# Picking embedding rows by one-hot products: tables in teams of two, with shared compares and two banks

## The reference

```python
e = jnp.stack([tbl_0[ids[:, 0]], ..., tbl_31[ids[:, 31]]], axis=1)   # 512 x 32 x 128
dot = jnp.einsum('bnd,bmd->bnm', e, e)
z = dot[:, iu, ju]                                                   # pairs above the diagonal
h = jnp.concatenate([z, dense_ctx], axis=1)                          # 512 x 512
h = jnp.maximum(h @ W_top1 + b_top1, 0.0)
h = jnp.maximum(h @ W_top2 + b_top2, 0.0)
y = h @ W_top3
```

## Time and profile before

| what | value |
|---|---|
| runs shown | 124.79, 125.47, 125.48 us, median 125.47 |
| span of the profiled execution | 148.7 us |
| own time of the profiled execution | not listed; the runs shown are other executions |
| TensorE (matmul) busy | 121.4 us, 82% of the span, 1028 instructions |
| ScalarE busy | 78.8 us, 53%, 79 instructions |
| VectorE busy | 75.2 us, 51%, 196 instructions |
| GpSimd busy | 71.3 us, 48%, 76 instructions |
| mean granted TensorE clock | 0.919 |

### The profile page before, as it was taken

How to read it: one execution, slowest core, us unless ns; L and a number is a source line. 1 busy time by engine, 2 the same in 40 slices (tenths; PEclk the granted TensorE clock), 3 DMA queues, 4 the chain that set the end, 5 groups by cost and what they waited for, 6 DMA issues and landing times.

```text
span 148.7 us, 2677 instructions
## 1 busy us (share of the span) xinstructions
PE 121.4 (82%) x1028; PEld 99.5 (67%) x1028; DVE 75.2 (51%) x196; ACT 78.8 (53%) x79; POOL 71.3 (48%) x76
## 2 busy tenths in 40 slices
PE   5889979989999689499995464321999899999993
PEld 3457758868788468378884452111999798999971
DVE  2999999989897399496800000000333033223301
ACT  3588899999997897799950510000143302210022
POOL 3877749787787477378775577772000000000000
PEclk9999999999999999959999776555599999999999
DMA  5998736666667356793221011211056441024000
GB/s 144 275 338 267 234 100 204 204 216 225 217 219 235 110 178 195 232 324 113 55 53 52 23 53 53 53 53 35 4 146 202 136 126 35 4 78 127 10 0 1
DMA packets 11150, 19.81 MB, mean 133 GB/s; under 512 B 2353, under 2 KB 7473, under 8 KB 11138
## 3 DMA queue, kind: packets, MB, share of 16 engines
q1 hardware_dynamic: 7522, 13.74, 29.8%
q0 software_dynamic: 2176, 4.46, 10.3%
q10 hardware_dynamic: 1440, 1.44, 3.0%
HBM read 17.54 MB, written 2.13 MB: 132 GB/s over the span
## 4 chain that ended last, share of the span: by engine, by line
PE 64%; ACT 15%; issue 11%; another core or an unknown queue 5%; DVE 2%; DMA 2%; ACTq 0%
PE two_ps L564 15%; PE two_ps L566 14%; PE two_ps L606 8%; PE two_ps L625 8%; ACT onehot L442 8%; PE free_ps L606 7%; ACT emb L421 5%; PE free_ps L636 3%; PE turn_ps L574 3%; PE two_ps L636 2%; ACT high L421 2%; DMA id_sb<-row_ids 2%; PE two_ps L641 1%; PE turn_ps L625 1%
## 5 line engine op out<-in xcount | busy, mean ns | idle before, releaser
L307 POOL DMA_INDIRECT rows<-tables,row_no x64 | 66.6, 1040 | 26.5 <-issue 14.9
L564 PE MATMUL two_ps<-onehot,high 128*128 128x512 f32 x128 | 52.7, 412 | 7.4 <-ACT onehot L442 4.3
L566 PE MATMUL two_ps<-onehot,low 128*128 128x512 f32 x128 | 50.9, 397 | 0.0
L442 ACT ACTIVATE onehot<-narrow 128x2560 fp32r<-128x2560 f16 (+3 forms) x16 | 35.5, 2226 | 4.8 <-PE two_ps L566 3.0
L564 PEld LDWEIGHTS two_ps<-onehot,high 128*128 128x128 f32 x128 | 24.8, 193 | 16.7 <-issue 10.4
L566 PEld LDWEIGHTS two_ps<-onehot,low 128*128 128x128 f32 x128 | 24.8, 194 | 4.7
L326 DVE TENSOR_SCALAR onehot<-pick_id,own_row 128x512 fp32r<-128x512 int16 x53 | 23.0, 479 | 4.4 <-PE two_ps L566 3.5
L316 DVE TENSOR_TENSOR low<-home,high 128x512 fp32r<-128x512 f32 (+1 forms) x36 | 22.4, 625 | 3.8 <-issue 3.7
L336 DVE TENSOR_SCALAR narrow<-pick_id,own_row 128x512 f16<-128x512 int16 x75 | 22.4, 365 | 0.0
L606 PE MATMUL two_ps<-emb 128*64 128x64 f32 x240 | 12.9, 247 | 9.4 <-issue 9.3
L196 DVE COPY home<-free_ps 128x512 f32<-128x512 f32 x4 | 2.8, 692 | 33.8 <-remote 29.8
(11 more groups left out here) (37 smaller groups left out, 54.5 us busy)
## 6 DMA issues: line engine op xcount, KB each, us to landing
home<-picked SPq DMA_DIRECT2D x10, 512.0 KB, 3.6
home<-picked SPq DMA_DIRECT2D x4, 640.0 KB
pick_id<-pick_ids SPq DMA_DIRECT2D x13, 128.0 KB, 3.7
w_sb<-w SPq DMA_DIRECT2D x3, 512.0 KB
dot_out<-home SPq DMA_DIRECT2D x10, 128.0 KB, 2.4
rows<-tables,row_no POOLq DMA_INDIRECT x64
dot_out<-home ACTq DMA_DIRECT2D x6, 128.0 KB, 2.6
pairs<-dot_out SPq DMA_DIRECT2D x10, 64.0 KB, 2.0
```

The source lines that it names most:

```text
L307: pool.indirect_dma_start(rows[:, k % ROWS_HELD, i, :], None, lone if one_table else tables, bass.IndirectOffsetOnAxis(ap=id_sb[:, 0, c:c ...
L442: act.activation(onehot[:, at:at + n, :], narrow[:, t % 2, n0:n0 + n, :], ACT.Copy).then_inc(onehot_act, n)
L564: pe.matmul(out, high[:, at, D * k:D * (k + 1)], onehot[:, c % HOT, :], start=(k == 0), stop=False)
L566: pe.matmul(out, low[:, at, D * k:D * (k + 1)], onehot[:, c % HOT, :], start=False, stop=(k == KR[t] - 1)).then_inc(picked_done, 1)
```

## The change

Table 0 stays alone, and tables 1 to 14 form seven teams of two (`TEAMS`), both of the same number of blocks. A *step* is one block of both tables of a team; there are 68 steps.

- One compare, 1024 wide, makes the one-hot rows of both tables of a step. `BY_ACT` now counts steps: three of eight go through ScalarE, four of ten.
- TensorE takes a step as four products: high and low of the first table in one bank, high and low of the second in the other.
- The ring holds 8 steps, which is as much memory as 16 blocks. Tables, ids and narrow rows are held for two teams (`HELD`).
- TensorE's tiles are turned in the middle and at the end of a team. In the last team, the last four blocks are done for the first table and then for the second (`SPLIT`); ScalarE copies the first table and 128 columns of the second, VectorE the other 384.
- `pace` counts steps instead of blocks, at the same share of the picks.
- The narrow rows get a larger buffer, `late`, in which later `h1`, `h2` and `y_row` lie. Layer 2's weights are loaded where the ids were, so their load waits for the last one-hot row.

The core of the diff:

```diff
+TEAMS = [[0]] + [[t, t + 1] for t in range(1, PICK, 2)]
-BY_ACT = [2, 4, 5, 5, 5, 5, 5, 5, 5, 5, 5, 6, 6, 6, 6]
+BY_ACT = [2, 3, 3, 3, 3, 3, 4, 4]
-TABLES_HELD, IDS_HELD, HOT, ROWS_HELD = 3, 4, 16, 7
+HELD, HOT, ROWS_HELD = 2, 8, 7
-        onehot = sb("onehot", [P, HOT, B], f32r)
+        onehot = sb("onehot", [P, HOT, 2, B], f32r)
+        late = sb("late", [P, HELD * NARROW * B], f32)
-        w2_sb = sb("w2_sb", [P, N1, H2], f32)
+        w2_sb = pick_id[:, :].bitcast(f32).rearrange("p (n h) -> p n h", n=N1)
...
-            def ids_load(t):
-                if t >= IDS_HELD:
-                    sp.wait_ge(onehot_dve, by_dve(t - IDS_HELD + 1))
-                    sp.wait_ge(narrow_ready, ACT0[t - IDS_HELD + 1])
...
+            for g in range(2, NT):
+
+                sp.wait_ge(onehot_dve, DVE0[g - HELD + 1])
+                sp.wait_ge(narrow_ready, ACT0[g - HELD + 1])
+                ids_load(sp, g)
+                table_load(g, 0)
+                table_load(g, 1)
...
-                    dve.tensor_scalar(onehot[:, c % HOT, :], pick_id[:, t % IDS_HELD, :], own_row[:, i, k:k + 1], None,
+                    dve.tensor_scalar(onehot[:, c % HOT, 0:n, :], pick_ids_of[:, g % HELD, 0:n, :],
+                                      own_row[:, STEPS.index(KT[g]), k:k + 1], None,
...
+            for g in range(1, NT):
+                if 1 < g < NT - 1:
+                    dve.wait_ge(pick_ids_in[g + 1], 16)
+                    make_narrow(g + 1)
+                if g >= HELD:
+                    dve.wait_ge(picked_done, STEP0[g - HELD + 1])
+                own = KT[g] - BY_ACT[g]
+                pieces = [(i, k0, k1) for k0, k1 in LOWS[g] for i in range(2)]
+                for j, (i, k0, k1) in enumerate(pieces):
+                    if k0 == 0:
+                        dve.wait_ge(high_ready, PIECES0 + 2 * (g - 1) + i + 1)
+                    split_low(g, i, k0, k1)
+                    if j:
+                        n = len(pieces) - 1
+                        make_onehots(g, DVE_K0[g] + own * (j - 1) // n, DVE_K0[g] + own * j // n)
...
+            for g in range(1, NT):
+                if g + 1 < NT:
+                    split_high(g + 1, 0)
+                    split_high(g + 1, 1)
+                if g >= 2:
+                    emb_out(2 * g - 4)
+                pick_out(g - 1)
+                if g + 1 < NT:
+                    make_onehots(g + 1)
+                if g >= 2:
+                    emb_out(2 * g - 3)
...
+            def pick(g, k0, k1):
+                for k in range(k0, k1):
+                    step_waits(g, k)
+                    for i in range(len(TEAMS[g])):
+                        last = row_block(g, i, k)
+                    last.then_inc(picked_done, 1)
```

More of the change, by code:

```diff
@@ L19 @@
 STEPS = sorted(set(KR))
+TEAMS = [[0]] + [[t, t + 1] for t in range(1, PICK, 2)]
+NT = len(TEAMS)
+KT = [KR[team[0]] for team in TEAMS]
+assert PICK % 2 and all(KR[t] == KT[g] for g, team in enumerate(TEAMS) for t in team)
+STEP0 = [sum(KT[:g]) for g in range(NT + 1)]
 PIECE = 2
 PIECES0 = KR[0] // PIECE
-LOW_CUT, HOT_CUT = [4, 4, 2], [3]
+LOW_CUT = [4, 4, 2]
 def cut(k, sizes):
@@ L247, in _ @@
             for j in range(PIECES0):
[L248 to L252, removed]
+                sp.dma_start(table[:, 0, 0, n * j:n * (j + 1)], first[:, n * j:n * (j + 1)]).then_inc(piece_in[j], 16)
+            table_load(1, 0)
+            table_load(1, 1)
+            for g in range(2, NT):
[4 more added lines that the diff above has]
+                table_load(g, 1)
             for r in range(BLOCKS):
@@ L424, in relu, with split_high @@
                 return act.activation(out, sums, ACT.Relu, bias=bias[:, n:n + 1])
-            def split_high(t):
+            def split_high(g, i):
+                t = TEAMS[g][i]
                 act.wait_ge(table_in[t], 16)
[L428 to L437, removed]
+                if g >= HELD:
+                    act.wait_ge(picked_done, STEP0[g - HELD + 1])
+                copy(high[:, g % HELD, i, 0:width(t)], table[:, g % HELD, i, 0:width(t)]).then_inc(high_ready, 1)
@@ L443, in make_onehots, with pick_out @@
                     n0 += n
[L445 to L453, removed]
+            def pick_out(g):
+                t0, n = TEAMS[g][0], len(TEAMS[g])
+                act.wait_ge(picked_done, STEP0[g + 1])
+                copy(emb[:, :, GF + t0:GF + t0 + n],
+                     two_ps[g % 2][:, 0:n, :].rearrange("p t b -> p b t")).then_inc(pick_emb_ready, 1)
@@ L648, in _ @@
                           start=True, stop=True)
-            for t in range(PICK):
-                pick(t)
-                if t >= LAG:
-                    turn(t - LAG)
+            pick(0, 0, KT[0])
+            for g in range(1, NT - 1):
+                if g >= 2:
+                    pe.wait_ge(pick_emb_ready, g - 1)
+                pick(g, 0, KT[g] // 2)
+                if g >= 2:
+                    turn(2 * g - 3)
+                pick(g, KT[g] // 2, KT[g])
+                turn(2 * g - 2)
+            g = NT - 1
+            pe.wait_ge(pick_emb_ready, g - 1)
+            pick(g, 0, KT[g] // 2)
+            turn(2 * g - 3)
+            pick(g, KT[g] // 2, SPLIT)
+            for k in range(SPLIT, KT[g]):
+                step_waits(g, k)
+                last = row_block(g, 0, k)
+            last.then_inc(picked_first, 1)
+            for k in range(SPLIT, KT[g]):
+                row_block(g, 1, k).then_inc(picked_done, 1)
+            turn(2 * g - 2)
             turn(TURNED - 1)
-            pe.wait_ge(pick_emb_ready, TWOS + 1)
+            pe.wait_ge(pick_emb_ready, NT + 1)
             dot_group(0)
```

195 lines of the change are left out of this document (88 added, 107 removed).

## The result

The changed kernel takes 132.0 us (median of 4 runs, 130.93 to 132.69), the kernel before 125.31 beside it (4 runs, 124.79 to 125.48). The ratio is 1.0555, 95% interval 1.0483 to 1.0627: slower by 6.7 us where 2.9 were forecast. The sign and the mechanism were forecast, the size was not.

A forecast was written before the change was run, and what follows sets the result against it. ScalarE was taken to set the pace of picking, by a hair. The last pick moves from 74.8 to 78.1 through five 2.2 us trips: 125.47 + 3.3 - 0.4 (split copy) = 128.4 us, range 122.8 to 132.5.

The forecast's parts named there:

- What was added: VectorE's queue: narrow rows wait for ids loaded only after the last full one-hot row, five times, some 2 us each.
- the size of the trip: Ids load of 256 KB, issue to use by VectorE: 2.2 us, bounds 1.7 and 3.7.
- The rest of the sum: Picking's other terms: team 1's rows end at 15.95, teams 6 and 7 take 9.67 and 9.56, last pick 78.1.
- VectorE's and ScalarE's share: Work per team of two: VectorE 6.9 us, ScalarE 6.3, both under TensorE's 8.2.
- The split copy: Last table's copy shared by ScalarE and VectorE: TensorE's 0.40 us wait after the last pick goes.
- the hold-ups are in the runs too: Rival, chance 0.22: ScalarE's idle times recur in the runs, earlier last pick 78.5, changed kernel 124.7 us.
- the trip is covered: Rival, chance 0.17, round trip short or covered: without any, TensorE paces, picks end at 71.6, in all 121.9.
- the trip is as long as the page's rows: Rival, chance 0.11: gathers collide with the ids loads, 3.7 us each, last pick 85.6, in all 135.9.
- the limit of 2.9: Trip length from which the long-trip rival decides against the forecast, 131.9 us; the forecast's case covers 1.9 to 2.9.
- The hole: First profile, 80.3 to 104.1 us: TensorE does little in 23.8 us; taken as absent from the runs shown.

The follow-up runs named there:

- the depth alone: Changed kernel with ids held four teams deep, in the place of the pair products, VectorE's order kept: 124.61 us, ratio to the kernel before 1.0013.
- the order alone: Changed kernel with the next team's narrow rows moved behind three lows and the full rows between them, depth two kept: 123.84 us, ratio 0.993.
- a longer trip: Changed kernel with each team's ids loaded behind its first table instead of ahead of both, in SP's order: 142.42 us (one run).
- the kernel before gets it with the depth alone: Kernel before, without teams or double rows, with ids held two tables deep instead of four: 139.3 us (one run).
- the trip taken apart above: Changed kernel with SP issuing a team's tables only when its ids have landed (tables held back): 132.41 us, ratio 1.0588.
- tile 14 moved: Changed kernel with narrow rows behind the lows, plus tile 14 turned and copied behind pair group 3 instead of group 0: 121.91 us, ratio 0.9757.
- the last team whole: Changed kernel without the split of the last copy, ScalarE copying both tables at once and VectorE none: 132.44 us, ratio 1.0607.

## Why the prediction was right and wrong

- **What was added: right.** Five waits of VectorE ahead of the narrow rows, ended by the load of the ids, and TensorE idle ahead of the teams. That they are the whole loss was shown four ways: the depth alone or the order alone removes it, a longer trip deepens it, and the kernel before gets it with the depth alone.
- **What failed: the size of the trip.** The forecast made it 1.25 until bytes flow, 0.9 for 256 KB, and 0.07 for the semaphores, which its sum counts once more: 2.27 from the last full row to the narrow rows. Measured are 2.8, 2.82, 2.72, 2.81 and 2.77, mean 2.78 (the first from the last full row's end at 16.32 to 19.12), 0.51 more each, 2.6 us over five. In the trip taken apart above the first bytes come after 0.95, earlier than forecast. It is the other two terms that were too small: the bytes took 1.38, not 0.9, since the load starts slowly, and from the last bytes to VectorE it took 0.36, where the forecast had only the 0.07. The theory that tables in tow make up the difference was tried and fell. Both terms go back to the reading of the earlier trace rows, half microseconds of a table and ids loaded together. I took the first stretch with full engines, from 30.0 on, for the start of the flow, and the emptying engines for the landing. The two stretches ahead of it, in the same trace, already hold the slow start (the last two columns are the share and GB/s):

```profile
29.00:29.50 0.50, 0.50 (x4) 0.41 (x3) 0.50 (x2) 0.50 (x2) 0.27 (x1) 1.00 0.44 66
29.50:30.00 0.50, 0.50 (x4) 0.42 (x3) 0.41 (x2) 0.50 (x1) 0.42 (x1) 1.00 0.66 123
```

- **The estimate by the Trainium skill was nearer.** The Trainium skill's "DMA: Bandwidth & Descriptors", section "Anatomy of one DMA — SWDGE (gpsimd) path", gives about 2.0 us fixed plus the bytes at 436 KB per us, fitted on the GpSimd path; this load is issued by SyncE. The estimate by it was 2.6 for this load and is 2.3 for 128 KB; the runs show 2.7 to 2.8 and 2.1, so it meets each time within 0.2 but has half the step between the two sizes (0.3 against 0.6 to 0.7). The forecast's sum with that estimate came out at 130.4, against 132.0 measured.
- **The rest of the sum.** The last full row of team 1 ended at 16.32, not 15.95 (+0.4). The last two teams took 19.7 us (61.72 to 81.45) where 19.2 were reckoned (+0.5). With 2.6 for the trips, that is the 3.4 between 78.1 and 81.45. The kernel before ended its picks 0.7 later than I had it. So the last pick moved by 6.0 us between the two profiled runs (75.46 to 81.45), not by 3.3, and the runs differ by 5.8 (125.12 and 130.93). The medians differ by 6.7; the profiled run of the change is the shortest of its four, and what made the others longer by 0.9 to 1.8 is not shown.
- **VectorE's and ScalarE's share: right.** A full double row takes 0.66 from start to start (31.40 to 32.06), a narrow one 0.40 (1.20 for three, 29.00 to 30.20), forecast 0.66 and 0.41. That the 0.66 is met so closely is luck in part: it was chosen between bounds of 0.60 and 0.73. ScalarE's waits for tables are not on the path: with the tables held back they rose from 13.4 to 20.1 us, and the time stayed.
- **The split copy: right,** 0.35 for a forecast of 0.40.
- **The rivals.** That the hold-ups are in the runs too: fell with the second profile of the kernel before. That the trip is covered: its floor, picks done at 71.6, is right for a kernel without the trip (72.5, 73.3), but not its total of 121.9, since TensorE then meets GpSimd's fetches. Only with tile 14 moved does 121.9 come, and that it is the very figure is luck, since that kernel differs from the forecast's also in what follows picking. That the trip is as long as the page's rows, 3.7: too long, but the measured trip lies nearer to the limit of 2.9 that I drew between the two cases than to my 2.27.

## What to carry to other kernels

When a buffer becomes shallower, look for the instruction that frees its place and the one that needs its next filling. If both stand next to each other in one in-order queue, a whole load from issue to use stands between them, in each round. Price that trip from a load that stands alone in a trace, from its issue to the consumer's first instruction, not from its bytes. Then either keep the depth or put work between the two; and when an engine gets faster by it, look at once for who is late next (here GpSimd's fetches), or the gain stays invisible.

## What the runs showed of the hardware that was not expected

- A load's landing hardly depended on what was issued behind it on the same queue: 2.8 us with 1 MB of tables in tow, 2.7 without. The tables did depend on what went ahead: 512 KB took 5.5 us behind the ids, and 4.5 with the ids landed first, measured in this profile:

```profile
home<-picked SPq DMA_DIRECT2D x10, 512.0 KB, 4.5
```

- Halving a load from 256 to 128 KB shortened it only from 2.7 or 2.8 to 2.1 us.
- At the start of a load the DMA engines can be busy and slow at once: a share of 0.83 at 106 GB/s, half a microsecond before 0.87 at 319. The load's packets of 2 KB took up to 0.53 us each there, and most of them 0.08 later.
- One load of 256 KB was used only 4.55 us after VectorE was ready for it, where its neighbours took 2.7 to 3.0 (the last team whole): eight of its 128 packets came late.
- One profiled execution can hold 23 us that the runs don't have. The hole and the hold-ups of the first profile did not return in another execution of the same kernel; what caused them stays open.
